# x by features from a second layout, reciprocal denominators spread by DMA, attention divided as it leaves PSUM, each V directly ahead of its A times V

## The reference, cut to what matters

```python
def attn(x, Wq, bq, Wk, bk, Wv, bv, Wo, bo):
    q = (x @ Wq.T + bq).reshape(b, t, H, DH).transpose(0, 2, 1, 3)   # k, v alike
    q = elu(q) + 1.0
    k = elu(k) + 1.0
    kv_cum = cumsum(einsum('bhtd,bhte->bhtde', k, v), axis=2)
    numerator = einsum('bhtd,bhtde->bhte', q, kv_cum)
    denominator = einsum('bhtd,bhtd->bht', q, cumsum(k, axis=2))
    out = numerator / maximum(denominator, 1e-6)[..., None]
    return out.transpose(0, 2, 1, 3).reshape(b, t, d) @ Wo.T + bo

def ffn(x, weight, bias):
    return mx_quantized(x) @ mx_quantized(weight).T + bias

x = x + layernorm(attn(layernorm(x), ...))
x = x + layernorm(ffn(layernorm(x), ...))
```

## Time and profile before

| | |
|---|---|
| median of 3 runs | 2441.12 us (2441.04 to 2442.33) |
| the profiled execution | 2443.11 us |
| its span in the profile | 2441.3 us |
| TensorE busy | 2402.6 us |
| VectorE busy | 1966.5 us |
| ScalarE busy | 1168.1 us |
| GpSimd busy | 1011.2 us |
| mean granted clock of TensorE | 0.995 of full speed |
| moved by DMA | 111.36 MB |

### The profile page before, as it was taken

How to read it: one execution, slowest core, us unless ns; L and a number is a source line. 1 busy time by engine, 2 the same in 40 slices (tenths; PEclk the granted TensorE clock), 3 DMA queues, 4 the chain that set the end, 5 groups by cost and what they waited for, 6 DMA issues and landing times.

```text
span 2441.3 us, 65347 instructions
## 1 busy us (share of the span) xinstructions
PE 2402.6 (98%) x27154; PEld 1972.1 (81%) x27154; DVE 1966.5 (81%) x4052; ACT 1168.1 (48%) x1965; POOL 1011.2 (41%) x1482
## 2 busy tenths in 40 slices
PE   6999999999999999999999999999999999999996
PEld 5888888888888888888888888888888888888885
DVE  7877888878888778888888887888888888878776
ACT  4544445544445444455444454444554444544442
POOL 1343344443444433444434444334444344443334
PEclk9999999999999999999999999999999999999998
DMA  4011011110111110111101111101111011111001
GB/s 159 27 46 53 28 36 53 45 53 27 36 53 53 45 53 27 36 53 45 53 28 36 53 54 45 54 27 36 53 45 53 28 36 53 53 45 53 27 19 44
DMA packets 59719, 111.36 MB, mean 46 GB/s; under 512 B 6816, under 2 KB 9248, under 8 KB 58912
## 3 DMA queue, kind: packets, MB, share of 16 engines
q1 hardware_dynamic: 59424, 107.18, 13.2%
HBM read 73.60 MB, written 33.55 MB: 44 GB/s over the span
## 4 chain that ended last, share of the span: by engine, by line
PE 97%; DVE 1%; DMA 0%; issue 0%; SPq 0%; ACT 0%; POOL 0%; POOLq 0%; DVEq 0%
PE work L354 15%; PE work L356 14%; PE work L355 14%; PE score L354 10%; PE score L356 9%; PE score L355 9%; PE work L373 8%; PE score L450 6%; PE work L485 5%; PE score L472 2%; PE state_bank L498 2%; PE work L425 1%; PE score L437 1%; DMA A<-in_wf 0%; SPq L322 0%
## 5 line engine op out<-in xcount | busy, mean ns | idle before, releaser
L997 DVE TENSOR_TENSOR A<-score,causal 128x512 f32<-128x512 f32 x512 | 317.8, 683 | 12.5 <-PE score L450 12.5
L1355 POOL TENSOR_TENSOR rs_f<-ve_f,minus_half 128x1 f32<-128x1 f32 x128 | 70.1, 547 | 598.3 <-DVE ve_f L914 598.3
L1365 POOL TENSOR_TENSOR x_res<-x_res,o_buf 128x512 f32<-128x512 f32 x128 | 179.0, 1398 | 153.3 <-ACT o_buf L626 151.9
L354 PE MATMUL work<-wv_hi,xT_hi 128*128 128x512 f32 x512 | 214.3, 419 | 1.6 <-issue 1.6
L354 PE MATMUL score<-xT_hi,wq_hi 128*128 128x512 f32 x512 | 207.1, 404 | 6.0 <-DVE KT L933 6.0
L354 PE MATMUL work<-wo_hi,oT_hi 128*128 128x512 f32 x512 | 208.1, 406 | 1.2 <-DVE oT_lo L1004 1.2
L354 PE MATMUL score<-xT_hi,wk_hi 128*128 128x512 f32 x512 | 206.3, 403 | 0.0
L356 PE MATMUL work<-wv_hi,xT_lo 128*128 128x512 f32 x512 | 201.4, 393 | 0.0
L355 PE MATMUL score<-xT_lo,wq_hi 128*128 128x512 f32 x512 | 200.8, 392 | 0.0
L356 PE MATMUL work<-wo_hi,oT_lo 128*128 128x512 f32 x512 | 200.6, 392 | 0.0
L355 PE MATMUL work<-wv_lo,xT_hi 128*128 128x512 f32 x512 | 200.6, 392 | 0.0
(11 more groups left out here) (138 smaller groups left out, 6339.0 us busy)
## 6 DMA issues: line engine op xcount, KB each, us to landing
x_in<-in_x SPq DMA_DIRECT2D x128, 256.0 KB, 4.4
x_res<-in_x SPq DMA_DIRECT2D x128, 256.0 KB, 2.9
out<-f_buf SPq DMA_DIRECT2D x96, 256.0 KB, 2.0
out<-xd SPq DMA_DIRECT2D x32, 256.0 KB, 2.1
V<-in_wk SPq DMA_DIRECT2D x4, 256.0 KB, 5.5
QT<-in_wq SPq DMA_DIRECT2D x1, 1024.0 KB, 5.9
kc<-in_wo SPq DMA_DIRECT2D x1, 1024.0 KB, 7.9
A<-in_wf SPq DMA_DIRECT2D x1, 1024.0 KB, 9.9
```

Of the source, the lines that this page charges most:

```text
L354: nc.tensor.matmul(dst, st_hi(c), mv_hi(c), start=(c == 0), stop=False)
L997: nc.vector.tensor_tensor(A[:, j, :, :], score_bank[j][:], causal[:].unsqueeze(1).to_broadcast([P, G, P]), ALU.mult).then_inc(a_set, 1)
L1355: nc.gpsimd.tensor_tensor(rs[n][:, b:b + 1], ve[n][:, b:b + 1], minus_half[:], ALU.pow).then_inc(rs_set[n], 1)
L1365: nc.gpsimd.tensor_tensor(x_res[:, b, :], x_res[:, b, :], o_buf[:, b % 2, :], ALU.add).then_inc(r_set, 1)
```

## The change

Four things, and a new order on every engine.

1. **x by features from a second layout.** The host hands over x a second time as `xt`, already by features ([sequence, tile, feature in group, group, token]). For tiles after the first, SyncE loads it into `exp_t` (`load_xt`), and GpSimd applies rs and shift there (`x_scale`: one multiplication, one addition per sequence, 128x512 each). In that layout a coefficient belongs to a column, so all partitions need all coefficients: `coef` (128 tokens x 2 x 4) is stored to DRAM and loaded back as a broadcast to 128 partitions, `x_coef` (`store_coef`, `spread_coef`, 512 KB). The transposes of xn and ScalarE's x_norm go; x_hi and x_lo read `exp_t` in SBUF instead of a PSUM bank, and x_hi waits for V of that sequence.
2. **Reciprocals spread by DMA.** `rinv` is stored to DRAM (64 KB) and loaded back four times (256 KB each) into `rden`, which now lies in the memory of `kc`. The 16 matmuls and the split of the reciprocals go.
3. **Attention divided as it leaves PSUM.** `divide` goes; past products and scores use the queries as they are. `normalise(b)` multiplies the attention of sequence b by its reciprocals, out of PSUM into `rden`; o_hi and o_lo read that.
4. **The order.** past products stand directly behind the last xd transposes, ahead of the denominators; V(0) stays ahead of scores(0), and V(1), V(2), V(3) each stand directly ahead of an o, in the turn of their own A times V.

The core of the diff:

```diff
 BANK_ORDER = [
-    (("v", 1), W1), (("v", 2), W2), (("v", 3), W0), (("x", 0), W1), (("att", 0), W2),
+    (("kn", 0), W0), (("f", 3), W1), (("att", 0), W2), (("kn", 1), W0), (("v", 1), W1),
...
+        rden = kc[:].rearrange("p g b t -> p (g b t)")[:, 0:NSEQ * D].rearrange("p (b n) -> p b n", b=NSEQ)
...
+            def load_xt(tile, b):
+                if b < 2:
+                    sp.wait_ge(q_set, count(tile - 1, G - 1))
+                else:
+                    sp.wait_ge(xT_set, count(tile, b - 2))
+                sp.dma_start(exp_t[:, b % 2, :], xt[b, tile].rearrange("p g t -> p (g t)")).then_inc(xt_loaded[b], 16)
...
+            def spread_coef(tile):
+                sp.wait_ge(coef_stored, 16 * tile)
+                if tile > 1:
+                    sp.wait_ge(x_shifted, count(tile - 2, NSEQ - 1))
...
+            def store_rden(tile):
+                sp.wait_ge(rden_set, count(tile, 0, 1))
+                sp.dma_start(rden_dram[:], rinv[:]).then_inc(rden_stored, 16)
+
+            def spread_rden(tile, b):
+                if b == 0:
+                    sp.wait_ge(rden_stored, 16 * (tile + 1))
+                src = rden_dram[b * DH:(b + 1) * DH, :].rearrange("(r j) t -> r (j t)", j=HPG)
+                sp.dma_start(rden[:, b, :], src.unsqueeze(1).to_broadcast([2 * G, DH // 2, HPG * P])
+                             ).then_inc(rden_loaded[b], 16)
...
                 xd_transposes(3)
+                past_products()
+                denominators()
                 v(0)
-                denominators()
+                scores(0)
                 kn(0)
                 f(3)
-                spread()
-                v(1)
-                past_products()
-                v(2)
-                scores(0)
-                v(3)
-                x_transposes(0)
                 attend(0)
                 state(0)
                 scores(1)
                 kn(1)
+                v(1)
                 if cur:
                     o(i, 0)
-                x_transposes(1)
                 attend(1)
...
+                def normalise(b):
+
+                    if cur:
+                        dve.wait_ge(rden_loaded[b], 16 * (i + 1))
+                        dve.wait_ge(att_mm, count(i, b))
+                        nc.vector.tensor_tensor(rden[:, b, :], bank(("att", b))[:], rden[:, b, :], ALU.mult).then_inc(o_scaled, 1)
...
+                def x_scale(tile, b):
+
+                    def by_token(k):
+                        return x_coef[:, :, k, b].unsqueeze(1).to_broadcast([P, G, P])
+
+                    rows = by_group(exp_t[:, b % 2, :])
+                    if b == 0:
+                        pool.wait_ge(coef_loaded, 16 * tile)
+                    pool.wait_ge(xt_loaded[b], 16 * tile)
+                    nc.gpsimd.tensor_tensor(rows, rows, by_token(0), ALU.mult).then_inc(x_scaled, 1)
+                    pool.wait_ge(x_scaled, count(tile - 1, b))
+                    nc.gpsimd.tensor_tensor(rows, rows, by_token(1), ALU.add).then_inc(x_shifted, 1)
```

595 lines of the change are left out of this document (301 added, 294 removed).

## The result

Median 2399.75 us (2394.48 to 2400.41, 4 runs) against 2441.08 us of the kernel before on the same chip: ratio 0.9825, 95% interval 0.9808 to 0.9842. The change makes the kernel faster by 41 us, where 90 were forecast (2351 us); 2399.75 lies above the range of 2344 to 2382 us. The profiled execution took 2399.21 us, its span is 2397.4 us, 48.4 us more than the 2349.0 of the sum.

What follows compares the result with a forecast made beforehand. TensorE, busy 98% of the span, bounds the kernel. 2.94 us per tile (88.2 us over thirty), plus first tile and end, takes 92.3 us from 2441.3; median about 2349, plus 2 for late hand-overs: 2351 us, range 2344 to 2382.

Steps and rivals of the forecast that it cites:

- TensorE's term: TensorE's work in each steady tile: 2.94 us less, 71.6 us instead of 74.56.
- the spread: TensorE's 16 matmuls that spread the reciprocals: their removal saves 0.60 us per tile.
- the x transposes: Four x transposes per tile on TensorE, behind the o products: removal saves 0.46 us each, 1.84 us together.
- the order: Each of V(1) to V(3) directly ahead of an o on TensorE: fewer lone products, 0.5 us saved per tile.
- The prediction's own sign of being wrong: Tile length from K(0) to K(0): the prediction is wrong if tiles last 73 us or more.
- The reciprocals' way: Reciprocals through DRAM to normalise(0): 6.1 us, 1 us more for transfers ahead; costs nothing, by about 1.5 us.
- rival C: Reciprocals land late before normalise(0): 5.3 us lost per tile, +73 us net, some 2514 us; chance beyond break-even 0.03.
- The waiter: VectorE's order, masks behind normalise(0), so attend(1) waits: tolerates reciprocals until 47.6 us in the tile.
- the band of 2375 to 2420: Whole-kernel time if x_scale is dear or VectorE waits for GpSimd, in full: chance 0.11.
- Rival A: GpSimd's x_scale takes 2.3 us, not 1.4: +34 us, 2385 us; up to 2.0 us shares 0.2, full shares 0.11.
- Rival B: VectorE's x_lo and o_lo wait out GpSimd instructions: about 1 us per tile, 2382 us; part shares 0.2, full 0.11.
- First tile and end: First tile gains some 4 us; the last tile gains 1.1 us, the drain loses 1 us.

Runs made afterwards that it cites:

- e1: The change without the reciprocals' trip through DRAM (store, four loads and waits left out; output wrong): 2373.38 us, ratio 0.9728.
- e12: The change with both x loads ahead of the second output store, the coefficients' broadcast behind the reciprocals' store, second residual load behind the reciprocals' loads: 2380.27 us.
- e9: The change with broadcast and first x load behind the reciprocals' store, second x load and second residual load behind the reciprocals' loads: 2450.36 us, ratio 1.0039.
- e6: The change with ScalarE's Kn(1) directly behind the seed of sequence 1, ahead of x_hi(0) and the second f norm: 2388.68 us, ratio 0.9784.
- e18: e12 with 30 past products repeated in the first tile and three or four last scores per tile, making tiles 6.5 times 256 instructions: 2361.62 us, ratio 0.9673.
- e11: The change with both x loads ahead of the second output store, second residual load behind the reciprocals' loads, GpSimd's first output sum behind its fourth dequantisation: 2382.09 us.
- e4: The change with the coefficients' broadcast replaced by a 512 KB load of distinct rows of x (coefficients wrong): 2400.28 us, ratio 0.9834.
- e3: e1 with the coefficients also stored and broadcast only once, not per tile: 2363.26 us, ratio 0.9685.

## Why the prediction was right in its sign and wrong in its size

- **TensorE's term: right within 0.15 us.** 2.94 us per tile were forecast. The best tile of the change is 71.78 us against 74.57, 2.79 us less, and in e1 most tiles have that length. Taken by the blocks' minima, the spread gave 0.60 us as forecast, the x transposes 1.94 instead of 1.84, the order 0.30 instead of 0.50; the xd transposes that now stand ahead of past products cost 0.17 us more. The prediction's own sign of being wrong was a tile of 73 us or more; the mean is 73.28.
- **The step that failed: "The reciprocals' way ... It costs nothing, by about 1.5 us."** The terms were 0.5 (queue), 2.2 (store), 0.45 and 2.9 us with 1 us for other transfers, 6.1 to 7.1 us. Measured as medians: 0.98 us to the store's issue, because it stands behind a residual load whose issue took up to 1.66 us and two x loads; 3.50 us until the loads are issued; 3.73 us until normalise(0): 8.2 us (the median of the whole way is 8.4, from 7.2 to 10.0). The 2.2 us came from a single 64 KB load at the start of the kernel; behind the residual load and the two x loads, 768 KB issued in the 1.6 us before, a 64 KB store took 3.5, and in e12 and e9, with only an output store 0.9 us ahead of it, 1.55 us until the loads could be issued. Against e12, what stands ahead in the queue costs 0.95 us of issue and 1.95 us of landing, 2.9 us for which the prediction had 1.5. That is rival C's mechanism at a seventh of its price: C had 5.3 us a tile, some 164 us, and the late sum is 23 (e1 gives 26 us of time).
- **The waiter was the wrong one.** The prediction looked at VectorE's order (masks behind normalise(0)) and there had 1.5 us of room: 47.6 less 39.1, 8.5 us for the whole way. The positions were good (reciprocal at 39.2 us in the tile instead of 39.1, attend(0) done at 46.2 instead of 45.9), and the ways measured go beyond 8.5 us by only 8.8 us over all 30 tiles; 23 were lost. The first to wait was o(0), for its bank, over ScalarE's order: o_hi(0) stands ahead of Kn(1), and e6, which changes that order alone, takes 10.9 of the 15.6 us there away. ScalarE was dismissed by its share: "busy for 48% as it is: nothing".
- **Not in the prediction at all: 21.9 us of instruction supply.** The reorder put past products, denominators and V(0) side by side; before, f(3) and more stood between the earlier trace rows, and no two of the places lay closer than 3.65 us. "So a tile is worth what TensorE's instructions take, as long as everything that TensorE waits for still comes in time" counted no wait for the instructions themselves, and fails where 256 of them take less than their load. e18 shows it.
- **The chances.** 2399.75 us lies in the band of 2375 to 2420 that had 0.11, but for rivals A and B; C, whose mechanism is half of what happened, had 0.03 and only beyond break-even.
- **Rival A (x_scale dear): no.** The multiplication of x_scale (the addition behind it takes 1.66 us in the mean) and the residual sum:

```profile
L1395 POOL TENSOR_TENSOR exp_t<-exp_t,x_coef x124: 1523/1622/1704, 61.5 to 2279.5; 128x512 f32<-128x512 f32 x124
```

```profile
L1402 POOL TENSOR_TENSOR x_res<-x_res,o_buf 128x512 f32<-128x512 f32 x128 | 175.6, 1372 | 104.5 <-ACT o_buf L670 104.5
```

  1.62 us instead of the 1.4 taken, inside the bounds, and off the path as long as x comes in time (e9 shows when not). The rule of the Trainium skill (GPSIMD Engine Reference, Performance pitfalls for Q7 kernels), half as much again, would have made it about 2.0 us by the prediction's estimate; the dearer part measured here is 0.32 us over the 1299 ns of the earlier trace rows, a quarter. The measurement decides.
- **Rival B (VectorE held by GpSimd): there, but free.** VectorE and GpSimd of the change, one quantisation and one output sum:

```profile
1141.86 1.72 DVE L1062 TENSOR_TENSOR q<-o_buf,rxs 128x512 fp8e4<-128x512 f32 x1
```

```profile
1141.35 1.68 POOL L1425 TENSOR_TENSOR f_buf<-f_buf,x_res 128x512 f32<-128x512 f32 x1 [0.61 <-ACT f_buf L670]
```

  The quantisation takes 1.72 us instead of its median 0.69: it ends 0.55 us after GpSimd's instruction does. 31 of the 32 last ones of a tile take that long, and oT_lo takes up to 2.20 us. The prediction called it unlikely from a product that took 0.75 us beside GpSimd, and that is where it misread its row: the first of GpSimd's two products ended at 1240.31, only 0.20 us after VectorE's product had begun, so 0.75 us is again an end 0.55 us after GpSimd's, and 31 of the 64 such products of the kernel before fit it. In the change all 81 quantisations and oT_lo that began with 0.15 us or more of a 128x512 instruction of GpSimd's to go ended 0.55 to 0.56 us after it. That is the Trainium skill's rule (SBUF, State Buffer: Two separate sides), and the traces agree: VectorE is blocked to the end. It is free because of where it falls, not because it is small. The hold on the quantisation costs VectorE 28 us and the kernel nothing (e11); no run takes the one on oT_lo away. x_lo, which the rival named too, never began during such an instruction in the change.
- **First tile and end.** The first tile was to gain 4 us and lost 1: the wait ahead of the spread went, but attend waited 1.97 us for its masks, and two Q products waited 3.94 and 2.87 us for VectorE's KT, where before one did, 6.04 us. The end was better by 5 us. That the two errors cancel in the total is luck. They are read from the traces alone; no run took them apart.

What stays open: what the hold on oT_lo, 22 us of VectorE's time in the change, is worth. That an instruction packet starts later while transfers run is seen, and that 512 KB of distinct rows do it as the broadcast does (e4); what it waits for, and when it is asked for, is not.

## What to carry to other kernels

Price a small transfer on the path by its place in the queue, with everything issued just ahead of it, and look along every engine's order for who stands behind its consumer: reordering four transfers here was worth 17 us. Where many short matmuls come together, count instructions, not only microseconds: a stop marked "issue" in mid-block, in the same tiles every time, was here the instruction stream running dry, and a tile length of 6.5 times the load's 256 held its places where they cost nothing, for 6.5 us of added work. And when "nothing else waits" depends on a free engine, check its order, not its share.

## What the runs showed of the hardware

- TensorE's instructions come in packets of 16 KB, about 256 instructions (52,292 matmuls and weight loads, 620 semaphore waits, 206 packets). In the change the packets of the eleven stops took 0.92 to 1.36 us, and work went on 1.28 to 1.53 us after they had landed.
- With at most 8 KB of other transfers in the stretch (e3), 256 instructions that take 1.8 to 2.4 us by themselves (the distance of two places less what the tile lost) made it stop, for up to 1.1 us; where they take 3.4 us it did not. With some 520 KB (the change) it also stopped where they take 3.4 to 4.0 us, and for up to 2.69 us.
- The stops of 2.24, 2.53 and 2.69 us of the change were each followed by a granted clock of 0.50 (the 1.2 GHz level) for 3.4 us, which cost 1.3 to 1.6 us more in V(0).
- A 64 KB store took 1.55 us (median) until the loads behind its landing were issued where only a 256 KB store stood 0.9 us ahead of it (e12), and 3.5 us behind three loads of 256 KB issued in the 1.6 us before (the change).
- VectorE's instructions with two SBUF inputs (quantisation, oT_lo, kc times q) that began during a 128x512 instruction of GpSimd's ended 0.55 us after it, whatever was left of it: 0.75 us in all with 0.20 us left, 1.72 with 1.17, 2.15 with 1.60.
